# The feed-forward's tail in a perceiver kernel: another order of its groups, scalings and projection pieces

## The reference

```python
x = x + _L0_xattn_ref(_layernorm(x), ctx_1024, Wq, Wk, Wv)
x = x + _L0_attn_ref(_layernorm(x), Wq, Wk, Wv)          # causal
x = x + _L0_ffn_ref(_layernorm(x), w1, conv_w, conv_b, w2)
x = x + _L1_xattn_ref(_layernorm(x), ctx_1024, W_kv, W_q, W_proj, b_proj)
x = x + _L1_attn_ref(_layernorm(x), Wq, Wk, Wv, W_O)
x = x + _L1_ffn_ref(_layernorm(x), router_w, gate_w, up_w, down_w)

# the feed-forward that the change is about
def act_quant(x):
    scale = 127.0 / clip(max(abs(x), axis=-1), 1e-05)
    return clip(round(x * scale), -128, 127) / scale
def bit_linear(x, w):
    return einsum('bsd,hd->bsh', act_quant(x), weight_quant(w))
h = bit_linear(x, w1)                       # 256 -> 1024
h = depthwise_conv1d(h, conv_w, conv_b)     # 3 taps along the sequence
out = bit_linear(silu(h), w2)               # 1024 -> 256
```

## Time and profile before

| | us |
|---|---|
| median of 3 runs | 2728.81 (2725.84 to 2732.73) |
| the profiled execution | 2730.85 |
| its span | 2729.1 |
| PE busy | 2525.6 |
| DVE, ACT, POOL busy | 1685.6, 1389.3, 838.3 |

### The profile page before, as it was taken

How to read it: one execution, slowest core, us unless ns; L and a number is a source line. 1 busy time by engine, 2 the same in 40 slices (tenths; PEclk the granted TensorE clock), 3 DMA queues, 4 the chain that set the end, 5 groups by cost and what they waited for, 6 DMA issues and landing times.

```text
span 2729.1 us, 75620 instructions
## 1 busy us (share of the span) xinstructions
PE 2525.6 (93%) x32404; PEld 2174.9 (80%) x32404; DVE 1685.6 (62%) x3003; ACT 1389.3 (51%) x2233; POOL 838.3 (31%) x857
## 2 busy tenths in 40 slices
PE   6999986789999999999999999999999976999997
PEld 3566655678888888888888888888888855999997
DVE  3467777436566565575665666755756555777775
ACT  1244443445555555555555555555556523555663
POOL 1010012343344434434334344344343300111111
PEclk9999997899999999999999999999999976999999
DMA  9886740560011001100100011011001102666664
GB/s 345 318 315 269 279 181 13 149 207 26 26 42 38 30 30 38 42 30 26 54 26 30 30 38 42 30 34 46 26 30 42 52 1 104 205 202 204 208 202 144
DMA packets 61265, 283.47 MB, mean 104 GB/s; under 512 B 5137, under 2 KB 36242, under 8 KB 46354
## 3 DMA queue, kind: packets, MB, share of 16 engines
...
## 4 chain that ended last, share of the span: by engine, by line
PE 58%; issue 12%; DVE 11%; DMA 7%; POOL 6%; ACT 5%; SPq 0%; POOLq 0%; DVEq 0%; ACTq 0%
PE PS L1450 7%; PE PS L1286 6%; PE PS L1274 5%; DVE mpart L1816 3%; PE PS L1195 3%; PE PS L1263 3%; PE PS L1261 3%; PE PS L1262 3%; PE PS L1446 3%; DMA unit_raw<-in_experts 3%; POOL ctx_lo L603 2%; PE PS L1170 2%; DMA sum_d<-scaled,xg 2%; PE PS L1252 2%; DVE sideB L1805 2%
## 5 line engine op out<-in xcount | busy, mean ns | idle before, releaser
L1816 DVE TENSOR_REDUCE mpart<-PS 128x1 f32<-128x802 f32 (+1 forms) x512 | 484.7, 986 | 213.7 <-PE PS L1274 212.7
L930 ACT ACTIVATE probs<-PS 128x1024 f32<-128x1024 f32 (+1 forms) x416 | 413.5, 1025 | 219.2 <-PE PS L1450 219.2
L603 POOL TENSOR_TENSOR ctx_lo<-ctx_raw,ctx_hi 128x801 fp32r<-128x801 f32 x128 | 227.8, 1790 | 381.5 <-ACT ctx_hi L865 372.9
L595 POOL TENSOR_TENSOR k_lo<-probs,k_hi 128x400 fp32r<-128x400 f32 (+1 forms) x256 | 250.9, 980 | 276.6 <-ACT k_hi L853 276.5
L1450 PE MATMUL PS<-qbd_hi,k_hi 64*128 64x256 f32 (+1 forms) x1664 | 314.8, 375 | 0.0
L1274 PE MATMUL PS<-k_hi,qbd_hi 128*128 128x512 f32 (+2 forms) x1024 | 266.0, 362 | 22.4 <-DVE mpart L1816 12.6
L852 ACT COPY probs<-PS 128x400 f32<-128x400 f32 (+1 forms) x256 | 126.3, 493 | 246.7 <-PE PS L1254 218.3
L1450 PE MATMUL PS<-qbd_lo,k_hi 64*128 64x256 f32 (+1 forms) x1664 | 235.5, 279 | 2.0 <-issue 2.0
L1261 PE MATMUL PS<-wkv_hi,ctx_hi 128*128 128x256 f32 (+1 forms) x832 | 237.3, 285 | 0.0
L1286 PE MATMUL PS<-probs,vals 128*32 128x64 f32 x13312 | 233.8, 221 | 2.7 <-issue 2.6
L1450 PE MATMUL PS<-qbd_hi,k_lo 64*128 64x256 f32 (+1 forms) x1664 | 235.3, 279 | 0.0
...
...
## 6 DMA issues: line engine op xcount, KB each, us to landing
...
```

The lines of the kernel that those rows point to most:

```text
L595: g.tensor_tensor(k_lo[:, n, a, c:c + width], k_raw[p % 2][:, 0:width], k_hi[:, n, a, c:c + width].bitcast(F32), ALU.subtract).then_inc(s. ...
L603: g.tensor_tensor(ctx_lo[:, a, cols], ctx_raw[:, cols], ctx_hi[:, a, cols].bitcast(F32), ALU.subtract).then_inc(s.ctx_lo_ready, 1)
L930: act.activation(probs[rows, t % PROBS, :], PS[rows, 1024 * (t % 2):1024 * (t % 2) + 1024], ACT.Exp).then_inc(s.pr_ready, 1)
L1816: v.tensor_reduce(mpart[:, pair, half:half + 1], PS[:, at:at + width], AX, ALU.max).then_inc(s.mx_red, 1)
```

## The change

Seven things move; the arithmetic stays.

- In the first attention ACT computes the exponential ahead of `copy_rows` (L803 behind L811), and PE does the row scales (`diag`) ahead of the hidden groups of its step.
- From chunk 6 on, the second to fourth groups go one step earlier on PE, so that groups 24 and 25, and 28 and 29, follow each other. The taps stay in their steps.
- In the tail DVE scales a chunk ahead of `xsT_lo` and the side taps of its step.
- In the tail `add_ffn` comes one step later (offset 18), and so there is one step more (FFN_STEPS).
- The pieces start at step 34, two earlier; the queries stay at step 35, now inside the same loop.
- ACT rounds the second context's first load behind the last piece (LAST_PIECES, step 41) and its second behind chunk 7's row scales (step 44). Before, both stood behind all steps.
- GpSimd makes the key remainders ahead of spreading the queries; ACT waits for the ones in `vals` only at the first value piece.

```diff
--- before.py
+++ after.py
@@ -45,7 +45,7 @@
 BPC = CHUNK // S
 HID_BUFS = 3
 GROUPS = HT // 2
-FFN_STEPS = 4 * CHUNKS + 14
+FFN_STEPS = 4 * CHUNKS + 15
 TAIL_GROUP = GROUPS * (CHUNKS - 2)
 UJ = HT // 2
 UW = 2 * KT * UJ * P + UJ * D
@@ -76,7 +76,9 @@
 PIECES = K_PIECES + V_PIECES
 PIECE_AFTER = (0, 2, 3, 4, 5, 7, 9, 10, 12, 13, 15)
 CTX_AT = {0: (0,), 2: (1,), 8: (2,), 10: (3,)}, {0: (0,), 2: (1,), 6: (2, 3)}
-BESIDE_FFN = [(2 * TILES + 4 + n, PIECES[2 * n:2 * n + 2]) for n in range(FFN_STEPS - 2 * TILES - 4)]
+BESIDE_FFN = [(2 * TILES + 2 + n, PIECES[2 * n:2 * n + 2]) for n in range(FFN_STEPS - 2 * TILES - 2)]
+LAST_PIECES = 2 * TILES + 2 + (len(PIECES) - 1) // 2
+LAST_ROWS = 4 * CHUNKS + 12
 PROBS = 4
 PLACES = KEY_TILES + 1
 S4_AT = (6, 8, 10, 12)
@@ -682,8 +684,8 @@
                 g.memset(vals[:, n, 0:(KEY_TILES - 1) * HEADS * VW].rearrange("p (t d) -> p t d", d=VW)[:, :, HD:VW], 1.0).then_inc(s.ones_ready, 1)
                 g.memset(vals[:, n, (KEY_TILES - 1) * HEADS * VW:], 1.0).then_inc(s.ones_ready, 1)
             split_queries()
+            split_keys(0)
             spread_queries(0)
-            split_keys(0)
             for part in range(KT * CTX_PARTS):
                 split_ctx(part)
             g.wait_ge(s.x_done, XDONE_F)
@@ -806,10 +808,10 @@
                 first, last = i == 0, i == TILES - 1
                 if not first:
                     copy_xsT()
-                copy_rows(2 * i)
                 act.wait_ge(s.nmax_ready, T["nmax"].up())
                 act.activation(probsA, PS[:, 2048:2048 + NK], ACT.Exp, bias=small[:, 1:2], scale=1 / 16,
                                accum_out=small[:, 2:3]).then_inc(s.probsA_ready, 1)
+                copy_rows(2 * i)
                 if not first:
                     copy_qkv()
                 act.wait_ge(s.pT_ps, 4 * i + 2)
@@ -950,21 +952,27 @@
             round_ctx(2)
             round_ctx(3)
             ffn(2 * TILES + 1)
-            ffn(2 * TILES + 2)
-            copy_xnT(7)
-            ffn(2 * TILES + 3)
-            query()
-            T["qbd"].up()
-            act.wait_ge(s.ones_ready, 4)
+            act.wait_ge(s.so_ps, TILES)
             pieces_evac[0] = 0
             for step, beside in BESIDE_FFN:
+                if step == 2 * TILES + 3:
+                    copy_xnT(7)
                 copy_rows(step)
                 ffn(step)
+                if step == 2 * TILES + 3:
+                    query()
+                    T["qbd"].up()
                 for piece in beside:
+                    if piece == V_PIECES[0]:
+                        act.wait_ge(s.ones_ready, 4)
                     evac(piece, 0)
-            T["k_lo"].up(len(K_PIECES))
-            for part in range(KT * CTX_PARTS):
-                round_ctx(part)
+                if step == LAST_PIECES:
+                    T["k_lo"].up(len(K_PIECES))
+                    round_ctx(0)
+                    round_ctx(1)
+                if step == LAST_ROWS:
+                    round_ctx(2)
+                    round_ctx(3)
             act_pair(True, False)
             with act.Fori(1, TILES - 1) as i:
                 enter("B", i, 1)
@@ -1126,14 +1134,16 @@
 
             def ffn(step):
 
-                for m in range(GROUPS):
-                    for f in chunk_at(step, 9 + m):
-                        hidden_group(GROUPS * f + m)
                 for f in chunk_at(step, 16):
                     pe.wait_ge(s.diag_ready, TPC * (f + 1))
                     for k in range(TPC):
                         mm = pe.matmul(bank(0, P, at=k * P), ones[:, :], diag[:, k, :], start=True, stop=True)
                     mm.then_inc(s.rows_ps, 1)
+                for f in range(CHUNKS):
+                    for m in range(GROUPS):
+                        ahead = 1 if m and f >= CHUNKS - 2 else 0
+                        if step == 4 * f + 9 + m - ahead:
+                            hidden_group(GROUPS * f + m)
                 for f in chunk_at(step, 8):
                     pe.wait_ge(s.xf_ready, TPC * (f + 1))
                     if f >= 2:
@@ -1470,12 +1479,13 @@
                 for n in range(2):
                     pe_batch(n, first, last, ranked)
 
-            prepare(QUERY_AT[0])
-            ffn(2 * TILES + 3)
-            prepare(QUERY_AT[1])
             count[0] = 0
             for step, beside in BESIDE_FFN:
+                if step == 2 * TILES + 3:
+                    prepare(QUERY_AT[0])
                 ffn(step)
+                if step == 2 * TILES + 3:
+                    prepare(QUERY_AT[1])
                 for piece in beside:
                     if piece == PIECES[0]:
                         pe.wait_ge(s.wkv_lo_ready, 1)
@@ -1730,14 +1740,19 @@
 
             def ffn(step):
 
+                tail = step >= 2 * TILES
+                if tail:
+                    for f in chunk_at(step, 16):
+                        scale_hidden(f)
                 for f in chunk_at(step, 8):
                     rest_of_xf(f)
                 for m in range(GROUPS):
                     for f in chunk_at(step, 9 + m):
                         side_taps(GROUPS * f + m)
-                for f in chunk_at(step, 16):
-                    scale_hidden(f)
-                for f in chunk_at(step, 17):
+                if not tail:
+                    for f in chunk_at(step, 16):
+                        scale_hidden(f)
+                for f in chunk_at(step, 18 if tail else 17):
                     add_ffn(f)
                 for f in chunk_at(step, 15):
                     hidden_steps(f)
```

## The result

Run beside the kernel before on one chip, the changed kernel took 2704.98 us (median of 4 runs, 2704.26 to 2709.3), the kernel before 2730.49 us (4 runs, 2725.84 to 2732.73): a ratio of 0.9909, with a 95% interval from 0.9897 to 0.9922. The forecast was 2702.5 us, so it is right in the sign and within 2.5 us in the size. The profiled execution has a span of 2702.4 us, 26.7 less than before, against 26.3 forecast. The page's first part shows that little of it is less work: PE's busy time fell by 8.1 us of 2525.6, and the other 18.6 us are idle time of PE that went.

A forecast was written before the change was run, and what follows sets the result against it. TensorE was busy 93% of the span, so time could be won only where it waits or runs slowly. 6.3 (first attention) + 20.0 (tail) = 26.3 us off, giving 2702.5 us against the median of 2728.81; range 2695 to 2713.

The forecast's parts named there:

- The first attention: Four tile pairs with a chunk at offset 16: exponential ahead of the row copy saves 4 x 1.57 = 6.3 us.
- Rival (c): First attention's gain swallowed, PE waiting for DVE or a load instead: 2708.8 us; chance 0.08.
- chunk 7's chain: Tail, through chunk 7's addition: batch stage starts at 482.5 in place of 502.50, 20.0 us gained.
- (1): Tail, from the attention's mask at 405.0 through chunk 4's scaling to DVE's normalising, ending at 419.7.
- (2): Tail, chunk 5's maxima, quantising, taps, steps and diag: 431.6, plus 1.6 of collisions with GpSimd, 433.2.
- (3): Tail, chunk 5's scaling and output to chunk 6's maxima, DVE waiting for a centring behind two evacuations: ends at 453.5.
- (4): Tail, chunk 6's scaling behind two value pieces at half clock (2.6 each) and the row copy: ends at 463.5.
- (5): Tail, chunk 6's output through chunk 7's maxima, scaling, output and addition: 481.3 to 483.0, taken as 482.3.
- context chain: Tail, ACT's rounding and GpSimd's splitting of the second context: ends at 480.5 or 481.7, so the 7.86 us wait goes.
- (a): PE at half clock through the tail and the chain from group 28 on: 9 us less gained, 2711.5 us; chance 0.12.
- (b): PE at full clock throughout the tail, saving 1.7 + 2.4 less 0.5: 2698.5 us; chance 0.10.
- (d): PE meets the batch stage at half clock and stays there; two batches cost 61: 2764 us; chance 0.04.

The follow-up runs named there:

- e1_rows_first: Changed kernel with ScalarE copying the rows of K ahead of a pair's first exponential again: 2706.38 us, ratio 0.9918 to the kernel before.
- e8_spread_first: Changed kernel with GpSimd spreading the queries ahead of splitting the keys: 2708.45 us, ratio 0.9899 to the kernel before.
- e9_centre_ahead: Changed kernel with ScalarE's centre taps of chunk 7's second group one step earlier: 2706.76 us, ratio 0.9894 to the kernel before.
- e3_ctx_last: Changed kernel with ScalarE rounding all four context parts behind all feed-forward steps again: 2716.81 us, ratio 0.9956 to the kernel before.
- e6_pieces_late: Changed kernel with the pieces two steps later again, first context rounding with the last of them: 2716.39 us, ratio 0.9931 to the kernel before.
- e10_fill: Changed kernel with 24 additional unused products on TensorE ahead of chunk 7's output: 2710.75 us, ratio 0.9909 to the kernel before.
- e12_centre_fill_early: Changed kernel with chunk 7's second-group centre taps a step earlier and 14, 6 and 12 unused products in the last three gaps: 2703.07 us, ratio 0.9882.

## Why the prediction was right, step by step

**The first attention.** 6.3 us forecast, 6.88 found: the transposes start 1.72 earlier in a pair, not 1.57, since the pass of PE ahead of them overlaps with them and no wait at all is left. The cause was named too narrowly. The prediction gave the 6.3 to the row copy alone, and "rows ahead of groups on PE" stood in its heading without a price; e1_rows_first shows that this order alone brings 3.7 of it. Rival (c), that the gain is swallowed, is out: both runs show it at the stage's end.

**The last tile.** "0.6 less" for scores that come earlier: in executions of nearly one clock it is 22.50 against 21.84 to 21.90 at the lower, and 21.08 and 21.21 against 20.3 to 20.5 at the higher, so 0.6 to 0.9. The other 1.4 of the 2.06 us is the clock of this one execution (0.92; 0.85 in the profile of before), and no merit of the change; six of the eleven runs with the changed order there had 0.84, and two with the old order had 0.92.

**The tail, chunk 7's chain.** Counted from the start of chunk 4's scaling (405.0 in the forecast, 396.97 measured):

| step | forecast | measured | missed by this step |
|---|---|---|---|
| (1) normalised | 14.7 | 15.9 | +1.2 |
| (2) chunk 5's diag | 28.2 | 30.1 | +0.7 |
| (3) maxima of chunk 6 | 48.5 | 50.5 | +0.1 |
| (4) scaling of chunk 6 | 58.5 | 59.8 | -0.7 |
| (5) addition of chunk 7 | 77.3 | 79.5 | +0.9 |
| start | 77.5 | 79.6 | -0.1 |

The rows of DVE, GpSimd and ScalarE behind this:

```profile
411.52 1.38 DVE L1605 TENSOR_SCALAR xn<-x,mv,rstd 128x256 f32<-128x256 f32 x1 [1.14 <-POOL rstd L558]
...
423.22 0.99 DVE L1717 TENSOR_SCALAR small<-small 128x2 f32<-128x2 f32 x1
...
424.33 0.74 DVE L1720 TENSOR_SCALAR small<-small 128x2 f32<-128x2 f32 x1
...
425.30 1.77 DVE L1724 TENSOR_SCALAR diag<-ident,small 128x128 f32<-128x128 f32 x2
...
441.25 0.87 DVE L1698 SCALAR_TENSOR_TENSOR hidden_f<-PS,convw,hidden_f 128x252 f32<-128x252 f32 x2 [4.61 <-ACT hidden_f L783]
...
460.47 3.75 DVE L1710 TENSOR_REDUCE hmax<-hidden_f 128x128 f32<-128x1024 f32 x2 [0.77 <-ACT hidden_f L797]
...
423.14 1.90 POOL L597 TENSOR_TENSOR k_lo<-probs,k_hi 128x402 fp32r<-128x402 f32 x2
...
425.24 1.75 POOL L597 TENSOR_TENSOR k_lo<-probs,k_hi 128x400 fp32r<-128x400 f32 x2 [0.20 <-ACT k_hi L855]
...
439.79 0.50 ACT L855 CAST k_hi<-PS 128x400 fp32r<-128x400 f32 x1
...
440.17 1.04 ACT L783 ACTIVATE hidden_f<-PS,convb,convw 128x256 f32<-128x256 f32 x2
```

(1): xn took 1.38 us where its shortest is 0.4; it lies beside GpSimd's clearing of vals. In the kernel before it had taken 1.35, and the prediction put in 0.4. (2): three of chunk 5's steps collide with the key remainders, not two: 0.99, 0.74 and 1.77 for what takes 0.17, 0.21 and 0.48 elsewhere, 2.6 us more, where the prediction had 1.6 from the earlier trace rows. The Trainium skill ("SBUF — State Buffer", "Who interferes with whom") lets whoever issues first hold the shared pair for the whole instruction. The trace agrees: GpSimd, which ran first, had its usual 1.90 beside the steps in e8_spread_first, while they waited; only the reciprocal between them kept its 0.17. The prediction's alternative, that the 1.6 might fall on GpSimd, did not come. (3): nearly exact, and the wait for a centring behind two evacuations was named; it is the 4.61 us above, and e9_centre_ahead shows most of it to be on the path. (4): the two value pieces ahead of the rows took 4.4 us (447.73 to 452.17), not 5.2; the granted clock was 0.60 in the first and 0.64 in the second, half clock for the most part, and full behind them. (5): the first output took 1.92 (1.9 to 3.6 had been left open), but hmax of chunk 7 waited 0.77 for ScalarE's silu part, and from its end to the scaling it took 4.18, not 3.4, as the transposes and rows of chunk 7 ran at half clock (0.69 and 1.22).

Of the 17.39 us, 7.21 lie in tail I and 10.18 in tail II. In tail II 6.9 are PE's wait for the context chain, and 3.3 are chunk 7's own chain: from chunk 6's scaling to the end of the addition it took 26.55 us before and 23.25 after, 1.55 of this the rounding to hq, which no longer lies beside GpSimd's split of the context. e3_ctx_last and e6_pieces_late give 8.45 and 9.45 of tail II back. In tail I the old order has 64.2 to 65.4 and the new one 56.1 to 60.9, and the scaling ahead of the taps is the one part that was shown to carry some of it. No run undoes the addition's later step alone.

So the tail gained 17.4 where 19.4 were due (20.0 less the 0.6 of the last tile): the collisions are the mis-sized term, 1.0 in (1) and 1.0 in (2), and the smaller misses of the other steps cancel. That the sum came out at 26.3 both times is luck in part: 2.0 too much in the tail, 0.6 too little in the pairs, and 1.4 of clock that the execution had and the change doesn't give. Tail I alone would have come out 0.9 us shorter or 3.9 us longer in the other executions of the same instructions.

**The context chain.** Forecast "a microsecond ahead of the add", measured 1.5. Counted as in the table, it ends at 78.0 where 75.5 to 76.7 had been forecast, and its lead stayed because the addition was late too. The prediction counts this chain from the last piece, but gives the pieces' place no part in the gain; e6_pieces_late shows that without it the chain is last again. The announced signs came: the batch stage starts at 476.57 (476 announced), behind the addition, with the clock at 0.79 over the tail.

**Rivals.** (a), half clock throughout, did not come: the outputs of chunks 5 and 6 took 1.92. But e10_fill's tail I, 3.9 us longer with the same instructions, shows that a part of it comes by chance. There GpSimd's key remainders came earlier, beside DVE's rounding of chunk 5 to hq (1.89 us in place of 1.23); PE stood idle for 2.77 us ahead of group 28, in place of 0.54, and then did this group at half clock. (b), full clock throughout, did not come either: the outputs of chunks 4, 5 and 6 took 1.92, but the granted clock was 0.82 over tail I and 0.71 over tail II. e12_centre_fill_early shows what the rest is worth: 1.5 us of tail II, up to where the context chain sets the end. The Trainium skill ("TensorE: Matmul & The Clock Gate", "Part 1: The HAM clock gate (the "warmup" mystery)") has activity release the throttle; in that run the trace agrees, 3.60 against 1.92 for one and the same output. (d), half clock carried into the batch stage, is out: 1.00 in its first 25 us, 0.94 before.
